# The last layer of a perceiver kernel, run inside the attention layer before it

## What is computed

```python
x = x + L3_attn(layernorm(x), Wq, Wk, Wv, Wo, bo)      # 16 heads of 64 over 32 rows, softmax / (sum + 1e-10)
x = x + L3_ffn(layernorm(x), packed_weight, weight_scale, bias)

def L3_ffn(x, packed_weight, weight_scale, bias):      # ternary weights, 4 of them packed in one integer
    enc = (packed_weight[None, :] >> [0, 2, 4, 6][:, None] & 3).reshape(-1)
    w = (enc - 1.0).reshape(256, 256) * weight_scale
    act_scale = 127.0 / maximum(max(abs(x), axis=-1), 1e-5)
    x_dq = clip(round(x * act_scale), -128.0, 127.0) / act_scale
    return x_dq @ w.T + bias
```

## Time and profile before

| | us |
|---|---|
| median of 3 runs | 3562.82 (3559.78 to 3569.31) |
| the profiled execution | 3566.51, of it 3564.7 in the span |
| attention loop with its preparation, up to x of tile 15 | about 3263 to 3521 |
| ternary layer and store | about 3521 to 3564.7 |

### The profile page before, as it was taken

How to read it: one execution, slowest core, us unless ns; L and a number is a source line. 1 busy time by engine, 2 the same in 40 slices (tenths; PEclk the granted TensorE clock), 3 DMA queues, 4 the chain that set the end, 5 groups by cost and what they waited for, 6 DMA issues and landing times.

```text
span 3564.7 us, 93169 instructions
## 1 busy us (share of the span) xinstructions
PE 3224.8 (90%) x39254; PEld 2674.3 (75%) x39254; DVE 2200.5 (62%) x5259; ACT 1308.8 (37%) x3224; POOL 1140.9 (32%) x1809
## 2 busy tenths in 40 slices
PE   7988659988997969999999889989999999998996
PEld 5866447547985758888888667768888878887894
DVE  5756643356675156666666577764444458887557
ACT  5643101333222224444444443333222346665221
POOL 6767134122013443333333343200000035554003
PEclk9999779999997989999999989999999999999997
DMA  5620357541003431111111100022112111111000
GB/s 166 200 70 4 109 192 243 176 134 50 3 25 113 91 85 49 50 47 49 47 47 42 57 2 2 3 68 95 59 60 71 65 49 50 50 50 61 3 3 28
DMA packets 211279, 246.58 MB, mean 69 GB/s; under 512 B 19412, under 2 KB 191184, under 8 KB 207920
## 3 DMA queue, kind: packets, MB, share of 16 engines
q1 hardware_dynamic: 203376, 230.39, 20.6%
q0 software_dynamic: 7488, 10.23, 1.6%
HBM read 221.51 MB, written 18.61 MB: 67 GB/s over the span
## 4 chain that ended last, share of the span: by engine, by line
PE 74%; DVE 12%; issue 6%; POOL 3%; ACT 3%; DMA 1%; SPq 0%; ACTq 0%; POOLq 0%; DVEq 0%
PE psum L189 44%; PE psum L3685 11%; PE psum L971 2%; PE psum L3935 2%; PE psum L955 2%; PE psum L3144 2%; PE psum L3245 1%; PE psum L3213 1%; PE psum L3925 1%; DVE l2a_ss L1662 1%; DVE g_xn L1669 1%; POOL l0a_ms L1180 1%; PE psum L3154 1%; PE psum L594 1%; DVE g_xn L258 1%
## 5 line engine op out<-in xcount | busy, mean ns | idle before, releaser
L245 POOL TENSOR_SCALAR g_rs<-g_mv 128x4 f32<-128x4 f32 x24 | 5.0, 210 | 771.2 <-DVE g_mv L378 770.7
L3685 PE MATMUL psum<-l2f_hhi,l2f_whi 128*128 128x512 f32 x512 | 199.3, 389 | 0.0
L3685 PE MATMUL psum<-l2f_hlo,l2f_whi 128*128 128x512 f32 x512 | 199.2, 389 | 0.0
L3685 PE MATMUL psum<-l2f_hhi,l2f_wlo 128*128 128x512 f32 x512 | 199.2, 389 | 0.0
L189 PE MATMUL psum<-l2x_kT,l2x_Qp 128*128 128x257 f32 x768 | 179.1, 382 | 2.7 <-ACT g_xn L3568 2.6
L3739 DVE CAST l2f_hhi<-l2f_tmp 128x512 fp32r<-128x512 f32 x96 | 41.0, 427 | 201.7 <-ACT l2f_tmp L3802 200.6
L189 PEld LDWEIGHTS psum<-l2x_kT,l2x_Qp 128*128 128x128 f32 x768 | 141.9, 191 | 21.9 <-issue 3.3
L3802 ACT ACTIVATE l2f_tmp<-psum,g_cols 128x512 f32<-128x512 f32 x64 | 44.2, 690 | 240.1 <-PE psum L3685 240.1
L3568 ACT ACTIVATE g_xn<-psum,l2x_sm 128x257 f32<-128x257 f32 x192 | 88.8, 472 | 90.7 <-DVE l2x_sm L3474 90.7
L4132 ACT ACTIVATE l3x_P<-psum,l3x_sm 128x257 f32<-128x257 f32 x256 | 117.6, 479 | 2.7 <-DVE l3x_sm L4054 2.7
L389 DVE TENSOR_TENSOR g_x<-g_x,psum 128x256 f32<-128x256 f32 x128 | 53.2, 416 | 99.1 <-PE psum L189 96.4
(11 more groups left out here) (890 smaller groups left out, 10632.8 us busy)
## 6 DMA issues: line engine op xcount, KB each, us to landing
l2f_raw<-L2f_h SPq DMA_DIRECT2D x64, 512.0 KB, 3.3
l0f_w<-L0f_w SPq DMA_DIRECT2D x23, 1024.0 KB
l0x_ctxT<-ctxT SPq DMA_DIRECT2D x64, 257.0 KB, 2.8
l1x_ctxT<-ctxT SPq DMA_DIRECT2D x64, 257.0 KB, 5.6
l0x_ctok<-ctx SPq DMA_DIRECT2D x64, 256.0 KB, 3.4
l1x_ctok<-ctx SPq DMA_DIRECT2D x64, 256.0 KB
l2x_cT<-ctxT SPq DMA_DIRECT2D x64, 256.0 KB, 2.8
l2x_tok<-ctx SPq DMA_DIRECT2D x128, 128.0 KB, 2.9
```

The source lines that it names most:

```text
L3685: t = e.matmul(z, a, b, start=c == 0 and u == 0, stop=c == 7 and u == 2)
```

## The change

`l3_ffn` and `final_store` go; the ternary layer becomes a class `TernaryFfn`, whose stages are put into the `ticks` of the last attention (`wide_attn(..., last=True)`) with lag 9 and up. It works on pairs of tiles: an item i does nothing when it is even, and handles pair u = i // 2 when it is odd.

- GpSimd, at the end of its tick: `norm` (lag 9: waits for the statistics; deviation, the two applies, then the bias add of the pair in one instruction) and `round` (lag 10: all of the quantisation, for pairs 0 to 6).
- VectorE, at the end of its tick: `unpack` in tick 1, `scale` (lag 10: the row maximum and the scale; for pair 7 also the applies and the quantisation), `total` (lag 11: the two adds to x).
- TensorE: `turn` (lag 11: four transposes) between project and the second parts, `project` (lag 11: four matmuls) at the end of the tick. Both take a bank of the same ring of two, so an even tick from 12 on takes it nine times.
- ScalarE: the copy of the transposes (lag 11).
- SP: the three small loads stand behind the attention's weights, and the store is in six transfers, of tiles 0 to 3, 4 to 7, 8 to 11, 12 and 13, 14, 15.

In between, the barrier ahead of the ternary layer is gone. Its arithmetic stays; the quantisation of pairs 0 to 6 is now GpSimd's, where only the last subtraction was.

```diff
-def wide_attn(K, pre, bias, eps, scale, keep, brow_name):
+def wide_attn(K, pre, bias, eps, scale, keep, brow_name, last=False):
+        ffn = TernaryFfn(K, sc, 9) if last else None
...
+            if key[0] in ("fT", "fy"):
+                return ffn.freed(key)
...
             load_rows(e, w_in[6], wo, A[pre + "_o"], split=4)
+            if last:
+                ffn.loads(e)
+                ffn.store(e, w)
...  (TensorE)
-                       (4, "a"): lambda i: p1(i, value(i, 0)), (4, "b"): lambda i: p1(i, value(i, 1)), **at.pe(e, w, banks, ready)},
-                  [2, (0, "a"), (4, "a"), 6, 7, (0, "b"), (4, "b"), (1, "row")])
+                       (4, "a"): lambda i: p1(i, value(i, 0)), (4, "b"): lambda i: p1(i, value(i, 1)), **at.pe(e, w, banks, ready),
+                       **(ffn.pe(e, w, take) if last else {})},
+                  [2, (0, "a"), (4, "a"), 6, 7] + [(11, "turn")] * last + [(0, "b"), (4, "b"), (1, "row")] + [(11, "project")] * last)
...  (GpSimd)
-            ticks(16, at.pool(e, w, (bb[:], bb_ok.at(1))), at.order)
+            ticks(16, {**at.pool(e, w, (bb[:], bb_ok.at(1))), **(ffn.pool(e, w) if last else {})},
+                  at.order + [(9, "norm"), (10, "round")] * last)
...  (VectorE)
+                  [2, (0, "a"), (4, "a"), (0, "c"), 5, 6, 7, (0, "b"), (4, "b"), (1, "row"), (0, "d")]
+                  + [(1, "unpack"), (10, "scale"), (11, "total")] * last)
...  (ScalarE)
+                  [(4, "power"), (0, "a"), (4, "a"), (0, "c"), 6] + [(11, "turn")] * last + [(0, "b"), (4, "b"), (0, "d")])
...
+class TernaryFfn:
+    def store(self, e, w):
+        for a, b in ((0, 4), (4, 8), (8, 12), (12, 14), (14, 15), (15, 16)):
+            w.wait_ge(self.x_out.at(b))
+            load(e, self.out, o[:, a:b, :], self.K.x[:, a:b, :])
+        w.wait_ge(self.out.now())
+    def by_pool(self, u):
+        return u < 7
+    def apply(self, e, u, k):
+        e.tensor_scalar(self.xn[u % 2][:, k, :], K.x[:, i, :], K.mv[:, i, 0:1], K.rs[:, i:i + 1], ALU.subtract,
+                        ALU.mult).then_inc(*self.xn_ok.up())
+    def quantize(self, e, w, u, step):
+        q = self.xn[u % 2]
+        for k in range(2):
+            e.tensor_scalar(q[:, k, :], q[:, k, :], self.am[:, 1, 2 * u + k:2 * u + k + 1], self.MAGIC, ALU.mult, ALU.add).then_inc(*step.up())
+        w.wait_ge(step.now())
+        e.tensor_scalar(q[:], q[:], self.MAGIC + 127.0, self.MAGIC - 128.0, ALU.min, ALU.max).then_inc(*step.up())
+        w.wait_ge(step.now())
+        if u >= 2:
+            w.wait_ge(self.turned.at(u - 1))
+        e.tensor_scalar(self.xq[u % 2][:], q[:], -self.MAGIC, None, ALU.add).then_inc(*self.xq_ok.up())
+    def freed(self, key):
+        return self.xqT_ok.at(key[1] + 1) if key[0] == "fT" else self.x_out.at(2 * key[1] + 2)
...
+        def norm(i):                                   # GpSimd
+            if i % 2 == 0:
+                return
+            u, sl = i // 2, slice(i - 1, i + 1)
+            w.wait_ge(K.sig("stat").at(i + 1))
+            e.tensor_scalar(K.rs[:, sl], K.mv[:, sl, 1], 1e-5, None, ALU.add).then_inc(*step.up())
+            w.wait_ge(step.now())
+            e.tensor_tensor(K.rs[:, sl], K.rs[:, sl], K.negh[:, 0:2], ALU.pow).then_inc(*self.rs_ok.up())
+            if self.by_pool(u):
...
+                for k in range(2):
+                    self.apply(e, u, k)
+            w.wait_ge(self.loaded)
+            w.wait_ge(self.xn_ok.at(2 * u + 2))
+            e.tensor_tensor(K.x[:, sl, :], K.x[:, sl, :], self.bb[:].unsqueeze(1).to_broadcast([128, 2, 256]), ALU.add).then_inc(*self.xb_ok.up())
```

More of the change, by code:

```diff
@@ L1443, in l3_attn @@
 def l3_attn(K):
-    wide_attn(K, "L3a", False, 1e-10, 0.125, False, "L3_attn_bo")
+    wide_attn(K, "L3a", False, 1e-10, 0.125, False, "L3_attn_bo", last=True)
 def l2_attn(K):
@@ new lines, in freed, with pe, turn, project @@
+    def freed(self, key):
+        return self.xqT_ok.at(key[1] + 1) if key[0] == "fT" else self.x_out.at(2 * key[1] + 2)
+    def pe(self, e, w, take):
+        def turn(i):
+            if i % 2:
+                u = i // 2
+                w.wait_ge(self.id_ok.at(1))
+                w.wait_ge(self.xq_ok.at(u + 1))
+                z = take("fT", u)[:, 0:256].bitcast(BF16)
+                for c in range(2):
+                    for k in range(2):
+                        n = 2 * c + k
+                        t = e.transpose(z[:, n * 128:(n + 1) * 128], self.xq[u % 2][:, k, c * 128:(c + 1) * 128], self.idb[:])
+                t.then_inc(*self.turned.up())
+        def project(i):
+            if i % 2:
+                u = i // 2
+                w.wait_ge(self.wb_ok.at(1))
+                w.wait_ge(self.xqT_ok.at(u + 1))
+                z = take("fy", u)
+                for k in range(2):
+                    t = matmuls(e, z[:, k * 256:(k + 1) * 256], [(self.xqT[u % 2][:, c, k, :], self.wb[:, c, :]) for c in range(2)])
+                t.then_inc(*self.y_ps.up())
+        return {(self.lag + 2, "turn"): turn, (self.lag + 2, "project"): project}
@@ new lines, in pool, with rounded @@
+    def pool(self, e, w):
+        K, step = self.K, self.step_p
+        e.tensor_copy(self.idb[:], K.ident[:]).then_inc(*self.id_ok.up())
+        def norm(i):
[7 more added lines that the diff above has]
+            if self.by_pool(u):
+                w.wait_ge(self.rs_ok.now())
+                if u >= 2:
+                    w.wait_ge(self.xq_ok.at(u - 1))
+                for k in range(2):
+                    self.apply(e, u, k)
+            w.wait_ge(self.loaded)
+            w.wait_ge(self.xn_ok.at(2 * u + 2))
+            e.tensor_tensor(K.x[:, sl, :], K.x[:, sl, :], self.bb[:].unsqueeze(1).to_broadcast([128, 2, 256]), ALU.add).then_inc(*self.xb_ok.up())
+        def rounded(i):
+            if i % 2 and self.by_pool(i // 2):
+                w.wait_ge(self.am_ok.at(i // 2 + 1))
+                self.quantize(e, w, i // 2, step)
+        return {(self.lag, "norm"): norm, (self.lag + 1, "round"): rounded}
@@ L4301, in program, with act, turn @@
+    def act(self, e, w, banks):
+        def turn(i):
+            if i % 2:
+                u = i // 2
+                w.wait_ge(self.turned.at(u + 1))
+                if u >= 2:
+                    w.wait_ge(self.y_ps.at(u - 1))
+                copy_act(e, self.xqT[u % 2][:].rearrange("p c k q -> p (c k q)"), banks.of(("fT", u))[:, 0:256].bitcast(BF16)).then_inc(*self.xqT_ok.up())
+        return {(self.lag + 2, "turn"): turn}
 def program(nc, A, out):
@@ L4305, in program @@
             layer(K)
[L4306 to L4320 removed]
 LAYERS = [("l0x", l0_xattn), ("l0a", l0_attn), ("l0f", l0_ffn), ("l1x", l1_xattn), ("l1a", l1_attn), ("l1f", l1_ffn),
[L4324 removed]
+          ("l2x", l2_xattn), ("l2a", l2_attn), ("l2f", l2_ffn), ("l3x", l3_xattn), ("l3a", l3_attn)]
 def lerp():
```

210 lines of the change are left out of this document (68 added, 142 removed).

## The result

| us | before | after |
|---|---|---|
| median of 20 runs each | 3566.05 (3557.91 to 3572.76) | 3559.16 (3551.16 to 3564.24) |
| the profiled execution, its span | 3566.51, 3564.7 | 3561.9, 3560.2 |
| last two layers in the trace | 301.5 | 291.2 |

The ratio is 0.9977, with a 95% interval of 0.9969 to 0.9985: faster by 8.2 us (5.3 to 11.1), and the two medians lie 6.9 us apart. The estimate is inside the 0.3% (10.7 us) that I had counted as no change; the end of its interval is not. As a difference, the forecast case (8.85 less) came about. As a time, 3559.16 is inside the stated range and 2.2 above that case's own 3551 to 3557. Of the 5 us between its 3554.0 and the 3559.16, 3.2 are the median of before, which had been 3562.82 in three runs.

The account below looks back on a forecast made before the run. TensorE was taken to bound the attention loop and VectorE the ternary layer behind it. Attention ending 8.0 us later, 22.5 of 39 us staying behind it and an end of 4.8 gave 8.85 less than 3562.82: 3554.0, range 3547 to 3562.

Parts of the forecast that it names:

- the forecast case: Whole kernel: 8.85 us less, 3554.0 us, with 3551 to 3557 as its own span; chance 0.47.
- the start phase: Start of the last attention: added loads and unpacking cost 0, up to 2 us if the loads come late.
- Ticks 12 to 16: Attention loop: bank wait for y's eviction 0.66 and projection 0.48, 1.14 us a tick, 3.4 for three ticks.
- Ticks 18 and 20: Late attention loop: VectorE late, pair 4's projection holding values(15), GpSimd's port contention 0.7 each; 4.6 us more.
- The third rival: Ticks 16, 18 and 20: L1041 and tiny tensor_scalars wait fully for the shared port, 2.8 us more, 3556.8; chance 0.08.
- Values(15) to x of tile 15: Last stretch of the attention: predicted unchanged, 0.
- The tail: From x of tile 15 to the last add: pairs 5 to 7 take 22.5 us of the old 39.
- The end: From VectorE's last instruction to the end of the span: 4.8 us with a smaller last store, before 5.13.
- The first: Rival, in the loop: TensorE pays only its own instructions, 0.7 us a tick, total 3547 to 3550; chance 0.22.
- The second: Rival: GpSimd's two-operation work costs what its single-operation form does, 4.4 us more, 3558.4; chance 0.12.
- The fourth: Rival: GpSimd bounds the last ticks, its late round holding the attention; 16 to 17 us more, 3571; chance 0.09.
- The fifth: Rival: the change does nothing, the same chain only split in pairs and as long as before; chance 0.02.

Follow-up runs that it names:

- e5: The changed kernel with all applies and all quantisation on VectorE, none on GpSimd; last two layers 301.73 us.
- e2: The changed kernel with all 16 of the attention's bias adds on GpSimd in tick 4, as before the change; last two layers 288.8 us.
- e4: The changed kernel with the applies and quantisation of pairs 5 and 6 on VectorE; last two layers 289.14 us, ratio to before 0.9971.
- e1: The changed kernel with the turn behind the first second part instead of in front, on TensorE and ScalarE; last two layers 291.39 us.
- e6: The changed kernel with the turn of pairs 0 to 2 in front of project instead of behind it; last two layers 290.90 us.
- e10: The changed kernel with GpSimd's apply written as add of the negated mean and multiply; last two layers 289.8 us.
- e7: The changed kernel with the applies and quantisation of pair 6 on VectorE, pair 5 staying on GpSimd; last two layers 287.30 us.
- e12: The changed kernel with early turn of pairs 0 to 2, add-and-multiply apply and two-operation last step on GpSimd; last two layers 286.49 us, ratio to before 0.9959.
- e8: The changed kernel with early turn of pairs 0 to 2 and pair 6 quantised by VectorE; last two layers 286.39 us, ratio to before 0.9959.
- e11: The changed kernel with a multiplication by 1.0 added to GpSimd's last quantisation step; last two layers 290.5 us.

## Why the prediction was right, point by point

**Bound and direction.** Right: the layer was a VectorE stage of 39 us behind the attention, and 22 of it stay. Ten us of TensorE's loop were paid for 17 of the tail.

**The sum: right in part by luck.** Three costs came out larger than priced: ticks 12 to 16 by 1.3 us, ticks 18 and 20 by 0.6, the stretch behind values(15) by 2.2. Against these 4.1 us stand a tail 0.5 and an end 2.6 shorter than priced, the latter mostly by a wait that I had no term for, and in the profiled pair 2.5 of the start phase, which is no gain of the change as far as is shown. Without the start phase the layer is 7.8 us shorter, near the 8.2 of the timing.

**Ticks 12 to 16: mis-sized.** The step was "VectorE reaches the add at 3455.09", 0.20 behind y. In tick 12 it was 0.79, and the tick cost 1.81 instead of 1.14. I had read one tick as the pattern of both; the issue gap of 0.46 in that tick was in the same view. Tick 14 cost 1.85 with the wait as priced; its surplus is the 0.6 of stops ahead of y, for which the sum had no term. Tick 16 cost 1.05.

**Ticks 18 and 20: near.** 5.2 instead of 4.6. Some 0.4 of it is the projection of pair 4 at the lower clock (1.01 us instead of 0.60). The port, of which I had taken 0.7 for each, shows only here and there. DVE timeline of after:

```profile
3503.15 0.36 DVE L1037 TENSOR_SCALAR l3a_nm<-l3a_nm 128x16 f32<-128x16 f32 x1
...
3512.91 0.75 DVE L1037 TENSOR_SCALAR l3a_nm<-l3a_nm 128x16 f32<-128x16 f32 x1
...
3520.45 0.55 DVE L1037 TENSOR_SCALAR l3a_nm<-l3a_nm 128x16 f32<-128x16 f32 x1
...
3521.33 0.89 DVE L1041 TENSOR_TENSOR l3a_P<-l3a_P,l3a_nm 128x512 f32<-128x512 f32 x1
```

L1037 is 0.17 and L1041 0.69 undisturbed. The rows are the divides of tiles 13, 14 and 15, in ticks 18, 19 and 20: 0.2, 0.6 and 0.6 us longer, 1.35 together. In e5, without GpSimd's applies and quantisation, L1037 stays at 0.17 and L1041 at 0.69 in every tick, so GpSimd's work is what lengthens them. The third rival's full wait, L1041 near 2.1, never came. The Trainium skill (GPSIMD Engine Reference, 1. Specifications) states that GpSimd shares its SBUF interfaces with VectorE, with contention for VectorE instructions in a 2-port mode or with two SBUF inputs; the trace agrees in the sign, at 0.2 us for L1041, which has two such inputs, where the earlier trace rows had shown 1.4.

**Values(15) to x of tile 15: a term left out.** I had it unchanged. Stretches of after and of e2, each ahead of values(15) and behind its start:

```profile
3518.00:3526.30 8.30, 5.86 (x163) 4.99 (x163) 7.27 (x18) 1.27 (x3) 3.57 (x6) 0.93 0.01 2
3526.30:3532.00 5.70, 5.70 (x146) 5.64 (x146) 2.85 (x5) 0.60 (x1) 4.15 (x4) 0.51 0.02 6
```

```profile
3514.80:3523.10 8.30, 5.76 (x162) 4.87 (x161) 7.71 (x20) 1.79 (x3) 3.21 (x5) 1.00 0.01 2
3523.10:3528.80 5.70, 5.70 (x164) 5.65 (x164) 3.95 (x9) 0.60 (x1) 4.51 (x5) 1.00 0.03 6
```

TensorE works without a break in the second line of each, at a granted clock of 0.51 in after, which is its 1.2 GHz level, and at 1.00, its 2.4 GHz level, in e2. Ahead of it TensorE was busy for 5.9 and 5.8 us of 8.3, where in before it had been 7.6. From values(15) to x of tile 15 it takes 9.6 to 10.0 us at the low level and 7.5 at the high one (e4 and e5, with more work on VectorE there, 11.8 and 12.5). The clock fell to the low level in six kernels (the changed one, e1, e4, e5, e6 and e10) and not in e2, e7 and e12; e8 and e11 lay between (0.70, and 9.0 and 8.8 us). It fell in none of the three kernels with the loop of before. The change opened the gaps ahead; whether the clock falls behind them varies, and costs up to 2.2 us. That the gaps are the cause is what this pattern suggests; no run here closes them alone.

**The tail: 22.0 instead of 22.5, with two errors that cancel.** The norm of a pair took 3.6 us and not 2.5 (applies at 1221), the round 3.2 and not 3.9 (L4200 at 478, the clip at 615). From the end of the quantisation to VectorE's add it was 2.3 for pair 5 and 2.5 for pairs 6 and 7, as priced. VectorE does wait there in order (DVE timeline of after):

```profile
3540.70 0.88 DVE L4313 SCALAR_TENSOR_TENSOR g_x<-psum,l3a_inv,g_x 128x256 f32<-128x256 f32 x2 [3.42 <-PE psum L189]
3542.07 0.69 DVE L4290 TENSOR_REDUCE l3a_am<-l3a_fxn 128x2 f32<-128x512 f32 x1 [0.50 <-POOL l3a_fxn L4194]
...
3549.66 0.88 DVE L4313 SCALAR_TENSOR_TENSOR g_x<-psum,l3a_inv,g_x 128x256 f32<-128x256 f32 x2 [5.25 <-PE psum L189]
```

The 0.50 is the longer norm, which I had as over in time.

**The end: mis-sized.** 4.8 taken, with bounds of 4.2 and 5.1; it was 2.27. I had looked at the landing and not at the wait for TensorE's queue beside it. The cause is open.

**The rivals.** The first (bare instructions) is refuted by the 0.86 us wait, and became real in tick 12 with e6. The second (single-operation prices) holds for the apply only, which even passes them (1221 ns against 958). Of the third (port) only 1.35 us came, about what the sum had for it. The fourth, GpSimd as the bound, didn't come: up to x of tile 15 TensorE never waits for GpSimd, which is busy 7.15 of tick 12's 16.1 us. The fifth is refuted by the tail.

## What to carry to other kernels

When a take is added to a two-bank ring, read in every tick that gets it how late the eviction ahead comes, and put it where the ring has rested, not where the code is tidy. Work moved to a second engine to cover a loop may be worth moving back to the faster one for the items that run when the loop is over; time it, since such an item can stand in the way of the loop's last steps (e4). Before an elementwise operation is called dear on GpSimd, write it in another pair of operations and measure that.

## What the hardware showed that I had not expected

- GpSimd's tensor_scalar on 128x256 f32: subtract and multiply 1221 ns, add and multiply 548, multiply and add 478. On 128x512: min and max 615, a lone addition to bf16 1504, the same with a multiplication by 1.0 617.
- The same instructions of the start phase took between 39.1 and 44.6 us to the scores of tick 4: 39.1 at a granted clock of 1.00 and without a stop, 42.4 at 0.91 with a stop of 1.03 us marked issue on TensorE, 44.6 at 0.83 with one of 2.31.
- Behind a stretch in which TensorE was busy for 5.3 to 5.9 of 8.3 us (4.2 in e5), its clock went to the 1.2 GHz level in some kernels and not in others that are nearly the same, and the work that followed filled it wholly.
- The end of the program waited 2.0 to 2.8 us for TensorE's queue in three kernels with the layer of before, and 0.2 in the changed one.
